# First g on VectorE, wqkv's low halves and fc2's maxima at other places, and q made with its units down the partitions

## Chip, core and metric

The kernel runs on one core of one Trainium2 chip. The metric is the device time of one execution in microseconds (us). Points in time are counted from the start of the profiled execution's span.

## The reference, cut to what matters

`x` is (4, 2048, 512). Both parts start from `xn`, the layer norm of `x`. Part one is a linear recurrence over the 2048 time steps, part two a feed-forward net with a layer norm of its own and quantised weights; the output is `x + s * silu(ffn(xn))`.

```python
q, k, v = xn @ Wq.T, xn @ Wk.T, xn @ Wv.T          # 128 units each
def step(M, qkv):                                    # over time
    r_t = q_t @ M.T
    M_new = 0.99 * M + v_t.T @ k_t / b
s = (r @ Wo.T) * sigmoid(gate)
h = layernorm(xn) * gamma + beta
y = silu(h @ dequant(fc1_q) + b1)                    # 512 -> 2048
z = y @ dequant(fc2_q) + b2                          # 2048 -> 512
out = x + s * silu(xn + 0.5 * z)
```

## The kernel before

**Tiling.** The 8192 rows are 16 chunks of 512 rows. A chunk is 4 tiles of 128 rows, each 32 time steps of the 4 sequences, so the recurrence is done tile by tile: within a tile by a masked 128x128 score matrix, between tiles by the memory `mem_t`. The normalised rows `g_rows` are turned by TensorE (line 410, the first chunk's by line 523) and split into two float16 halves `g_hi` and `g_lo`; `h_hi`, `h_lo` are the feed-forward input, split by GpSimd (lines 1016, 1020). The weights `wqkv` and `q2` are split into halves too.

**Slots.** The order of all work after the start is written out by hand as slots, 64 for a chunk, and every engine walks the same slots in its own queue, with semaphores between them. In each slot TensorE does one step of fc1 (`ffn1`, line 466, two matmuls of 512 columns) and one of fc2 (`ffn2`, line 484, two matmuls), which runs 16 slots behind. ScalarE rescales fc1's sum between steps (line 603) and makes the silu (line 610), VectorE splits it into `y_hi` and `y_lo` (lines 708, 713) and rescales fc2's sum (line 722). fc1 needs slots 0, 2, 4, 6 for the even blocks and 5, 7, 9, 11 for the odd ones.

**Side jobs.** `SIDE` places the recurrence between them. Tile i of a chunk has `qkv` at slot 1 + 12 i (line 427: 12 matmuls with 128 rows of g held and 384 columns of weights passing), `qkt` 4 slots later (lines 432 and 433: q and k transposed), `scores` at +7 (line 436), `read` at +10 (lines 443 to 445, where 443 waits for VectorE's `mask_scores`, line 697, at slot 9 + 12 i) and `wo` at +13 (line 451). The turns of the next chunk are at slots 51, 54, 56 and 59. ScalarE copies the results out one slot behind (`qkv_copy`, `qkt_copy`, `r_copy`, `s_copy`); the scale of a row goes into q, k and v there. Side jobs alternate between two PSUM banks, and each waits until the job two before it has been copied out.

**The start.** Before slot 0, VectorE takes the maxima of wqkv and of q1 (line 760, 2048 elements in 2.28 us), GpSimd works out the row scales (`rows`, lines 978 to 988) and normalises the first chunk (`normalise`, line 1004), TensorE turns it, ScalarE copies it out as `h_full` (line 565) and `g_hi` (line 556), and VectorE makes `g_lo` (line 692) and `wqkv_lo` (line 872). Slot 0 of TensorE waits for `q1_scale`; its first `qkv` waits for `wqkv_split` and for all of `g_lo`.

**fc2's weights.** They are converted in chunk 0, in 16 pieces that share the two buffers of `wide`: GpSimd widens piece n at slot 14 + 3 n (`q2_widen`, line 1031), VectorE rounds it a slot later (`q2_high`, line 796), GpSimd makes the rest at two slots later (`q2_low`, line 1036). First the scale must be there: VectorE's maxima at slots 0, 1, 5 and 9, `pick` at slot 12, `largest` and `q2_scale` at slot 13. The ratio rows of fc2 (`ratio2`, held at slot 2) go through DRAM. The next chunk's `rows` stand on GpSimd at slot 28 in chunk 0 and at slot 7 in the others.

## Time and profile before

| | us |
|---|---|
| median of 3 runs (1291.27 to 1292.08) | 1291.49 |
| the profiled execution | 1291.07 |
| its span, first to last instruction | 1289.2 |
| TensorE busy | 1204.1 (93%) |
| VectorE busy | 1132.0 (88%) |
| ScalarE busy | 906.9 (70%) |
| GpSimd busy | 805.4 (62%) |

TensorE's mean granted clock is 0.986 of full speed. In the chain of work that ended last, TensorE has 77% of the span, VectorE 11%, issue 5%, ScalarE 3%, GpSimd 3%. A matmul's duration overlaps with that of the next, so the pace of TensorE is read from the starts.

### The profile page before, as it was taken

The numbers are of one execution on the slowest core, as the hardware profiler recorded it, in microseconds if no ns is written. First come the engines' busy times: TensorE is split into PE (matmuls) and PEld (weight loads), VectorE is DVE, ScalarE is ACT, GpSimd is POOL, SyncE is SP. The second block draws the span as 40 slices with busy tenths as digits, with TensorE's granted clock in tenths as the row PEclk, the third lists the DMA queues.
The fourth block names the chain that finished last, engine by engine and source line by source line (L and its number), as shares of the span: only waits on it lengthen the run. The fifth ranks groups of instructions, "written<-read, shape, count | busy, mean of one in ns | idle before, by whom it ended". The sixth has DMA issues, their size and how long they took to land.

```text
span 1289.2 us, 18645 instructions
## 1 busy us (share of the span) xinstructions
PE 1204.1 (93%) x5900; PEld 608.0 (47%) x5900; DVE 1132.0 (88%) x1962; ACT 906.9 (70%) x1558; POOL 805.4 (62%) x766
## 2 busy tenths in 40 slices
...
DMA packets 41620, 65.68 MB, mean 51 GB/s; under 512 B 11696, under 2 KB 11952, under 8 KB 41008
## 3 DMA queue, kind: packets, MB, share of 16 engines
...
q10 hardware_dynamic: 288, 0.08, 0.0%
...
## 4 chain that ended last, share of the span: by engine, by line
PE 77%; DVE 11%; issue 5%; ACT 3%; POOL 3%; DMA 1%; SPq 0%; DVEq 0%; POOLq 0%; ACTq 0%
PE blk L466 28%; PE blk L484 27%; PE side L427 10%; DVE blk L722 5%; PE side L451 4%; DVE y_split L713 2%; PE side L443 2%; DVE y_split L708 1%; PE side L410 1%; DVE g_lo L692 1%; PE side L444 1%; PE side L445 1%; PE side L436 1%; POOL g_rows L1004 1%; ACT blk L603 1%
## 5 line engine op out<-in xcount | busy, mean ns | idle before, releaser
L722 DVE TENSOR_TENSOR blk<-blk,ratio_rows 128x512 f32<-128x512 f32 x960 | 644.9, 690 | 88.9 <-PE blk L484 85.3
L603 ACT ACTIVATE blk<-blk,ratio 128x512 f32<-128x512 f32 x768 | 508.1, 666 | 228.5 <-PE blk L466 218.6
L466 PE MATMUL blk<-h_split,q_sb 128*128 128x512 f16 x2048 | 613.8, 382 | 10.2 <-issue 4.9
L484 PE MATMUL blk<-w_sb,y_split 128*128 128x512 f16 x2048 | 610.6, 380 | 6.5 <-DVE blk L722 4.3
L484 PEld LDWEIGHTS blk<-w_sb,y_split 128*128 128x128 f16 x2048 | 199.4, 98 | 253.5 <-DVE blk L722 14.1
L466 PEld LDWEIGHTS blk<-h_split,q_sb 128*128 128x128 f16 x2048 | 196.3, 98 | 223.9 <-issue 36.3
L610 ACT ACTIVATE y_full<-blk,par,last 128x512 f32<-128x512 f32 x256 | 201.3, 786 | 112.4 <-PE blk L466 112.3
L713 DVE SCALAR_TENSOR_TENSOR y_split<-y_full,up,y_split 128x512 f16<-128x512 f32 x256 | 218.8, 855 | 0.0
L1016 POOL CAST h_split<-h_full 128x512 f16<-128x512 f32 x64 | 52.9, 826 | 251.5 <-ACT h_full L565 251.5
L708 DVE TENSOR_SCALAR y_split<-y_full,up 128x512 f16<-128x512 f32 x256 | 159.4, 623 | 5.0 <-ACT y_full L610 5.0
L1004 POOL TENSOR_SCALAR g_rows<-xt,mv,gs 128x512 f32<-128x512 f32 x64 | 141.5, 2218 | 0.1
L1061 POOL TENSOR_TENSOR z_rows<-z_rows,xz 128x512 f32<-128x512 f32 x62 | 92.4, 1499 | 49.2 <-DVE z_rows L727 47.9
L1067 POOL TENSOR_TENSOR z_rows<-z_rows,s_rows 128x512 f32<-128x512 f32 x62 | 91.8, 1480 | 34.6 <-ACT z_rows L618 34.6
L1056 POOL TENSOR_TENSOR xz<-xz,b_half 128x512 f32<-128x512 f32 x64 | 88.4, 1382 | 5.3
L1070 POOL TENSOR_TENSOR z_rows<-z_rows,x_again 128x512 f32<-128x512 f32 x62 | 84.8, 1367 | 4.9
L427 PE MATMUL side<-wqkv_hi,g_hi 128*128 128x384 f16 x256 | 85.1, 332 | 1.8 <-DVE g_lo L692 1.8
L427 PE MATMUL side<-wqkv_lo,g_hi 128*128 128x384 f16 x256 | 85.1, 332 | 0.0
L427 PE MATMUL side<-wqkv_hi,g_lo 128*128 128x384 f16 x256 | 85.1, 332 | 0.0
L1020 POOL TENSOR_TENSOR h_split<-h_full,h_split 128x512 f16<-128x512 f32 x64 | 76.6, 1197 | 5.2
L727 DVE SCALAR_TENSOR_TENSOR z_rows<-blk,unit,ratio_rows 128x512 f32<-128x512 f32 x64 | 47.6, 746 | 32.2 <-PE blk L484 32.2
L451 PE MATMUL side<-wo_sb,r_t 128*128 128x512 f32 x128 | 65.4, 592 | 0.0
L1053 POOL TENSOR_SCALAR xz<-x_again,row_z 128x512 f32<-128x512 f32 x64 | 60.8, 950 | 0.2 <-POOL z_rows L1061 0.2
...
## 6 DMA issues: line engine op xcount, KB each, us to landing
...
x_again<-in_x SPq DMA_DIRECT2D x256, 64.0 KB, 1.9
out<-z_rows SPq DMA_DIRECT2D x256, 64.0 KB, 1.7
w_sb<-in_q SPq DMA_DIRECT2D x4, 1024.0 KB, 13.8
ratio_rows<-ratio_dram SPq DMA_DIRECT2D x4, 1024.0 KB, 7.6
y_split<-in_q SPq DMA_DIRECT2D x1, 1024.0 KB, 10.5
h_split<-in_q SPq DMA_DIRECT2D x1, 1024.0 KB, 12.7
z_rows<-in_q SPq DMA_DIRECT2D x1, 1024.0 KB, 14.6
```

The source lines that it names most:

```text
L427: mm = pe.matmul(bank[:, 0:QKV], a[:, k, rows], w[:, k, :], start=(k == 0 and n == 0), stop=(k == KC - 1 and n == 2))
L451: pe.matmul(bank[:], r_t[:], wo_sb[:], start=True, stop=True).then_inc(wo_done, 1)
L466: mm = pe.matmul(blk[J % 2][:], q1_sb[:, g, j // 4, w, j % 4 * P:(j % 4 + 1) * P], a[:, c % 2, g, :], start=(g == 0 and n == 0), stop=(g = ...
L484: mm = pe.matmul(blk2[:, i, :], y[:, J % Y_RING, rows], w2_sb[:, j, part, :], start=(j == 0 and n == 0), stop=(j == FB - 1 and n == len(te ...
L603: act.activation(blk[J % 2][:], blk[J % 2][:], ACT.Copy, scale=ratio1[:, at:at + 1]).then_inc(blk_scaled, 1)
L610: act.activation(y_full[:, J % 2, :], blk[J % 2][:], ACT.Silu, bias=b1_c[:, j:j + 1], scale=last1[:, j:j + 1]).then_inc(silu_done, 1)
L708: dve.tensor_scalar(y_hi[:, J % Y_RING, :], y_full[:, J % 2, :], up_y, None, ALU.mult).then_inc(y_hi_done, 1)
L713: dve.scalar_tensor_tensor(y_lo[:, J % Y_RING, :], y_full[:, J % 2, :], up_y, y_hi[:, J % Y_RING, :], ALU.mult, ALU.subtract).then_inc(y_l ...
L722: dve.tensor_tensor(blk2[:, i, :], blk2[:, i, :], ratio2_rows[:, j, :], ALU.mult).then_inc(blk2_scaled, 1)
L1004: pool.tensor_scalar(g_rows[:, i, :], xt[:, i, :], mv[:, c % 2, i, 0:1], gs[:, c % 2, i:i + 1], ALU.subtract, ALU.mult).then_inc(g_done, 1)
L1061: pool.tensor_tensor(z_rows[:, i, :], z_rows[:, i, :], xz[:, i % 2, :], ALU.add).then_inc(z_sum, 1)
L1067: pool.tensor_tensor(z_rows[:, i, :], z_rows[:, i, :], s_rows[:, n % S_RING, :], ALU.mult).then_inc(z_mul, 1)
```

## The change

Four things are altered.

1. **First g.** Chunk 0's four normalisations leave GpSimd (line 1004) for VectorE (`first_normalise`), behind `pick(OF_WQKV)` and ahead of `largest(OF_WQKV)`.
2. **Order at the start.** ScalarE makes `wqkv_hi` behind `h_full` and `g_hi` instead of ahead; VectorE makes `wqkv_lo` last, behind the scale and flag of q1 and all four `g_lo`; q1's last maximum moves ahead of the first `g_lo`.
3. **fc2's weights.** Maxima at slots 0, 1, 3, 5, ratios at 6, scale at 10 and 11, pieces from slot 12 (each two slots earlier than before).
4. **q.** A new job `q` at slot 3 of each chunk makes q of all four tiles at once and already transposed: the weights are held and the 512 rows of g pass, 12 matmuls of 512 columns. `kv` takes the place of `qkv` with 256 columns, `kt` that of `qkt` with one transpose. q can't be scaled by row any more, so `s_copy` scales by a third row factor, which GpSimd makes in `row_scales`; `s_mask` and `r_t` share one buffer, so `mask_scores` waits for `wo_done`.

```diff
-QKV_LAG, QKT_LAG, R_LAG, S_LAG, GHIGH_LAG, HFULL_LAG = 1, 1, 1, 1, 1, 2
+Q_AT = 3
+Q_LAG, KV_LAG, KT_LAG, R_LAG, S_LAG, GHIGH_LAG, HFULL_LAG = 1, 1, 1, 1, 1, 1, 2
-RATIO2_AT, TOP_Q2_AT, Q2_SCALE_AT = 2, (0, 1, 5, 9), 12
-Q2_AT = tuple(14 + 3 * n for n in range(FB))
+RATIO2_AT, TOP_Q2_AT, Q2_SCALE_AT = 6, (0, 1, 3, 5), 10
+Q2_AT = tuple(12 + 3 * n for n in range(FB))
...
+                elif job == "q":
+                    for k in range(KC):
+                        for n, (a, w) in enumerate(((g_hi, wqkv_hi), (g_lo, wqkv_hi), (g_hi, wqkv_lo))):
+                            mm = pe.matmul(bank[:], w[:, k, 0:M], a[:, k, :],
+                                           start=(k == 0 and n == 0), stop=(k == KC - 1 and n == 2))
+                    mm.then_inc(q_done, 1)
...
-                            mm = pe.matmul(bank[:, 0:QKV], a[:, k, rows], w[:, k, :],
+                            mm = pe.matmul(bank[:, 0:2 * M], a[:, k, rows], w[:, k, M:],
...
-                    pe.transpose(bank[:, 0:P], qkv[:, i % 2, 0:M], ident[:])
-                    pe.transpose(bank[:, P:2 * P], qkv[:, i % 2, M:2 * M], ident[:]).then_inc(qkt_done, 1)
+                    pe.transpose(bank[:, 0:P], kv[:, i % 2, 0:M], ident[:]).then_inc(kt_done, 1)
...
+            def q_copy(c, i, bank):
+                act.wait_ge(q_done, c + 1)
+                wait(act, read_done, 4 * c)
+                act.activation(q_t[:], bank[:], ACT.Copy, scale=in_c[:, 0:1]).then_inc(q_out, 1)
...
-                act.activation(s_rows[:, n % S_RING, :], bank[:], ACT.Copy, scale=powers[:, 0:1]).then_inc(s_out, 1)
+                act.activation(s_rows[:, n % S_RING, :], bank[:], ACT.Copy,
+                               scale=row_c[:, c % 2, 2, i:i + 1]).then_inc(s_out, 1)
...
+            def first_normalise(i):
+                if i == 0:
+                    dve.wait_ge(rows_done, 1)
+                dve.tensor_scalar(g_rows[:, i, :], xt[:, i, :], mv[:, 0, i, 0:1],
+                                  gs[:, 0, i:i + 1], ALU.subtract, ALU.mult).then_inc(g_done, 1)
...
-                wait(dve, read_done, 4 * c + i)
+                wait(dve, wo_done, 4 * c + i)
...
             rows(0)
-            for i in range(NT):
-                normalise(0, i)
             row_scales(0)
```

VectorE in the start, around the maximum of wqkv; before:

```order
L764 TENSOR_REDUCE top_col<-side 32x1
L765 TENSOR_SCALAR top_diag<-ident,top_col 32x32
L771 TENSOR_REDUCE top_wqkv<-side 128x1
L856 TENSOR_SCALAR bound<-top_wqkv 128x1
L857 TENSOR_SCALAR pow<-bound 128x1
L859 RECIPROCAL up<-pow 128x1
L860 TENSOR_SCALAR up<-up 128x1
```

and after:

```order
L792 TENSOR_REDUCE top_col<-side 32x1
L793 TENSOR_SCALAR top_diag<-ident,top_col 32x32
L712 TENSOR_SCALAR g_rows<-xt,mv,gs 128x512 x4
L799 TENSOR_REDUCE top_wqkv<-side 128x1
L886 TENSOR_SCALAR bound<-top_wqkv 128x1
L887 TENSOR_SCALAR pow<-bound 128x1
L889 RECIPROCAL up<-pow 128x1
```

Four normalisations have come in between the maximum and its use; on GpSimd the same four rows are gone.

TensorE in chunk 0, from the end of the first tile's `qkv` (slot 1) to the scores (slot 8); before:

```order
L427 MATMUL side<-wqkv_hi,g_lo 128x384
L427 MATMUL side<-wqkv_lo,g_hi 128x384
L466 MATMUL blk<-h_split,q_sb 128x512 x6
L432 MATMUL side<-ident,qkv 128x128
L433 MATMUL side<-ident,qkv 128x128
L466 MATMUL blk<-h_split,q_sb 128x512 x6
L436 MATMUL side<-qk_t 128x128
```

and after, from the end of `kv` into the new job `q` (`blk` is fc1's sum, `side` the side jobs' banks):

```order
L439 MATMUL side<-wqkv_hi,g_lo 128x256
L439 MATMUL side<-wqkv_lo,g_hi 128x256
L479 MATMUL blk<-h_split,q_sb 128x512 x2
L428 MATMUL side<-g_hi,wqkv_hi 128x512
L428 MATMUL side<-g_lo,wqkv_hi 128x512
L428 MATMUL side<-g_hi,wqkv_lo 128x512
```

Each `qkv` has lost a third of its columns, and 12 matmuls of 512 columns stand at slot 3.

GpSimd in chunk 0, at the end of `rows` and `row_scales` of chunk 1 (slot 28); before:

```order
L988 TENSOR_TENSOR row_z<-v,row_const 128x4
L996 TENSOR_TENSOR row_c<-v,in_c 128x4 x2
L1031 TENSOR_SCALAR xz<-w_sb,up 128x512
L1036 TENSOR_TENSOR w_sb<-xz,w_sb 128x512
L1031 TENSOR_SCALAR xz<-w_sb,up 128x512
```

and after:

```order
L1018 TENSOR_TENSOR row_z<-v,row_const 128x4
L1026 TENSOR_TENSOR row_c<-v,in_c 128x4 x2
L1026 TENSOR_TENSOR row_c<-v,powers 128x4
L1065 TENSOR_TENSOR w_sb<-xz,w_sb 128x512
L1060 TENSOR_SCALAR xz<-w_sb,up 128x512
L1065 TENSOR_TENSOR w_sb<-xz,w_sb 128x512
```

Behind the row scales GpSimd now finishes a piece and then widens the next, where it widened one at once; that next widening is piece 6 and not piece 5.

## Rows read from the trace of the kernel before

**Rows 1.** Busy time per engine in 76 us of steady work: PE, PEld, DVE, ACT, POOL.

```profile
207.00:283.00 76.00, 74.83 (x375) 38.27 (x374) 68.50 (x119) 56.25 (x99) 49.83 (x47) 1.00 0.17 42
```

**Rows 2.** TensorE's waits from 200 to 1200: line, releaser, total us, times, longest.

```profile
PE side L443 <- issue: 7.7, 13, 0.6
```

**Rows 3.** TensorE in time, one chunk's start: start, duration, [idle before, releaser].

```profile
513.22 0.33 PE L427 MATMUL side<-wqkv_hi,g_hi 128*128 128x384 f16 x1
...
515.17 0.59 PE L466 MATMUL blk<-h_split,q_sb 128*128 128x512 f16 x2
...
518.71 0.27 PE L432 MATMUL side<-ident,qkv 128*128 128x128 f32 x1
...
518.93 0.59 PE L466 MATMUL blk<-h_split,q_sb 128*128 128x512 f16 x2
519.36 0.59 PE L484 MATMUL blk<-w_sb,y_split 128*128 128x512 f16 x2
...
523.90 0.59 PE L484 MATMUL blk<-w_sb,y_split 128*128 128x512 f16 x2
525.09 0.46 PE L443 MATMUL side<-qk_t,mem_t 128*128 128x128 f32 x2 [0.59 <-issue]
```

**Rows 4.** VectorE in time, the mask for that read.

```profile
524.71 0.28 DVE L697 TENSOR_TENSOR s_mask<-side,mask 128x128 f32<-128x128 f32 x1
```

**Rows 5.** Chain of waits, tiles 1 and 2 of chunk 0: start, us, piece.

```profile
57.55 3.84 PE side L427 x12
...
77.22 1.95 PE side L427 x12
```

**Rows 6.** All engines in time, the start.

```profile
17.54 8.27 POOL L1004 TENSOR_SCALAR g_rows<-xt,mv,gs 128x512 f32<-128x512 f32 x4
...
25.87 1.12 PE L523 MATMUL blk<-ident,g_rows 128*128 128x128 f32 x4 [0.94 <-POOL g_rows L1004]
27.29 0.61 POOL L1016 CAST h_split<-h_full 128x512 f16<-128x512 f32 x1 [1.16 <-ACT h_full L565]
...
27.81 0.69 DVE L692 TENSOR_TENSOR g_lo<-blk,g_hi 128x512 f16<-128x512 f32 x1 [3.94 <-ACT g_hi L556]
...
31.67 1.80 DVE L872 SCALAR_TENSOR_TENSOR wqkv_lo<-s_rows,up,wqkv_hi 128x1536 f16<-128x1536 f32 x1
...
34.40 0.15 DVE L882 TENSOR_SCALAR q_shift<-up 128x1 f32<-128x1 f32 x1
...
36.10 1.01 PE L466 MATMUL blk<-h_split,q_sb 128*128 128x512 f16 x2 [3.67 <-issue]
...
37.55 0.50 PE L427 MATMUL side<-wqkv_hi,g_hi 128*128 128x384 f16 x1 [0.44 <-DVE g_lo L692]
```

**Rows 7.** Page, costliest groups: VectorE's y_hi, count, busy us, mean ns.

```profile
L708 DVE TENSOR_SCALAR y_split<-y_full,up 128x512 f16<-128x512 f32 x256 | 159.4, 623 | 5.0 <-ACT y_full L610 5.0
```

**Rows 8.** All engines in time, slots 6 to 16 of chunk 0.

```profile
46.59 0.78 ACT L610 ACTIVATE y_full<-blk,par,last 128x512 f32<-128x512 f32 x1
...
55.96 0.63 PE L497 MATMUL blk<-top_diag,ones 32*128 32x32 f32 x2 [2.81 <-DVE top_diag L765]
...
64.72 0.59 PE L466 MATMUL blk<-h_split,q_sb 128*128 128x512 f16 x2 [1.19 <-issue]
```

**Rows 9.** Page, DMA issues: KB each, median us from issue to landing.

```profile
ratio_rows<-ratio_dram SPq DMA_DIRECT2D x4, 1024.0 KB, 7.6
```

**Rows 10.** All engines in time, slots 28 to 65 of chunk 0.

```profile
89.93 0.69 POOL L1031 TENSOR_SCALAR xz<-w_sb,up 128x512 f32<-128x512 int32 x1
...
90.65 0.43 DVE L796 CAST w_sb<-xz 128x512 f16<-128x512 f32 x1 [4.45 <-POOL xz L1031]
...
91.75 0.60 PE L484 MATMUL blk<-w_sb,y_split 128*128 128x512 f16 x2 [3.07 <-DVE blk L722]
...
94.76 0.77 PE L443 MATMUL side<-qk_t,mem_t 128*128 128x128 f32 x2 [2.41 <-issue]
...
137.82 0.32 PE L427 MATMUL side<-wqkv_hi,g_hi 128*128 128x384 f16 x1 [1.32 <-DVE g_lo L692]
```

More of the change, by code:

```diff
@@ L208, in build @@
         xz = sb("xz", [P, 2, H], F32)
-        qkv = sb("qkv", [P, 2, QKV], F32)
-        qk_t = sb("qk_t", [P, 2 * P], F32)
-        s_mask = sb("s_mask", [P, P], F32)
-        r_t = sb("r_t", [P, P], F32)
+        kv = sb("kv", [P, 2, 2 * M], F32)
+        q_t = sb("q_t", [P, T], F32)
+        k_t = sb("k_t", [P, P], F32)
+        s_mask = r_t = sb("s_mask", [P, P], F32)
         mem_t = sb("mem_t", [P, M], F32)
@@ L442, in run_side @@
                     wait(pe, mem_done, 4 * c + i)
-                    pe.matmul(bank[:, 0:P], mem_t[:], qk_t[:, 0:P], start=True, stop=False)
-                    pe.matmul(bank[:, 0:P], qkv[:, i % 2, 2 * M:3 * M], s_mask[:], start=False, stop=True)
-                    pe.matmul(bank[:, P:2 * P], qkv[:, i % 2, M:2 * M], qkv[:, i % 2, 2 * M:3 * M],
+                    pe.matmul(bank[:, 0:P], mem_t[:], q_t[:, i * P:(i + 1) * P], start=True, stop=False)
+                    pe.matmul(bank[:, 0:P], kv[:, i % 2, M:], s_mask[:], start=False, stop=True)
+                    pe.matmul(bank[:, P:2 * P], kv[:, i % 2, 0:M], kv[:, i % 2, M:],
                               start=True, stop=True).then_inc(read_done, 1)
@@ L589, in s_copy @@
                 n = 4 * c + i
-                if c == 0 and i == 0:
-                    act.wait_ge(decay_done, 1)
                 if n < S_RING:
@@ L637, in _ @@
                 q1_piece(n, 1.0, minus_point[:, 0:1])
-            act.wait_ge(wqkv_scale, 1)
-            act.activation(wqkv_hi[:], wqkv_in, ACT.Copy, scale=up_wqkv).then_inc(wqkv_hi_done, 1)
             for k in range(KC):
@@ L642, in _ @@
                 g_high(0, k, first_turn_bank[k])
+            act.wait_ge(wqkv_scale, 1)
+            act.activation(wqkv_hi[:], wqkv_in, ACT.Copy, scale=up_wqkv).then_inc(wqkv_hi_done, 1)
             act.wait_ge(q1_scale, 1)
@@ L661, in _ @@
                     q1_piece(FB // 2 + Q1_AT.index(G), up_q1, q1_shift[:, 0:1])
[L662 to L665 removed]
+                if at := job_behind(G, Q_LAG, "q"):
+                    q_copy(*at, side[JOB_BANK[G - Q_LAG]])
+                if at := job_behind(G, KV_LAG, "kv"):
+                    kv_copy(*at, side[JOB_BANK[G - KV_LAG]])
+                if at := job_behind(G, KT_LAG, "kt"):
+                    kt_copy(*at, side[JOB_BANK[G - KT_LAG]])
                 if at := job_behind(G, R_LAG, "read"):
@@ L854, in _ @@
             pick(OF_WQKV)
+            for i in range(NT):
+                first_normalise(i)
             largest(OF_WQKV, top_wqkv[:])
@@ L888, in _ @@
             g_low(0, 3, first_turn_bank[3])
+            dve.wait_ge(wqkv_hi_done, 1)
+            dve.scalar_tensor_tensor(wqkv_lo[:].rearrange("p k n -> p (k n)"),
+                                     wqkv_in.rearrange("p k n -> p (k n)"), up_wqkv,
+                                     wqkv_hi[:].rearrange("p k n -> p (k n)"), ALU.mult, ALU.subtract
+                                     ).then_inc(wqkv_split, 1)
             def q1_parts():
```

83 lines of the change are left out of this document (40 added, 43 removed).

## The prediction, made before the changed kernel ran

> **What bounds the kernel now.** I read the page's busy shares first, then the busy time by window, the waits of TensorE, one chunk of its timeline, and last the start. In 76 us of steady work TensorE is busy for 74.83, VectorE for 68.50, ScalarE for 56.25 and GpSimd for 49.83 [rows 1]: TensorE is the bound, and VectorE stands close behind it. So in chunks 1 to 15 a microsecond taken from TensorE's work comes off the end, as long as VectorE keeps up. The one named wait of any size there is that of the chunk's first read, 13 times, 7.7 us in all [rows 2]. Its cause is VectorE: the mask ends at 524.99 and the read starts at 525.09 [rows 3, 4]. VectorE is late there because the turns' low halves (slots 54 to 62) and the next chunk's statistics (slots 0 to 6) come on top of its usual work, while TensorE has only 1.95 us of side work in slots 1 to 4. The matmul ahead of the read started at 523.90, and a pair takes 0.43 (518.93 to 519.36), so the read could have started at 524.33: the wait costs 0.76 us a chunk [rows 3].
>
> Chunk 0 is another regime. Up to 37.55 the chain goes through GpSimd, ScalarE and VectorE, with TensorE waiting [rows 6]. From slot 12 to 65 fc2's weight pieces tie GpSimd and VectorE together, and TensorE runs dry several times [rows 8, 10]. After such gaps it runs at the lower of its two clock levels, 1.2 instead of 2.4 GHz: the 12 matmuls of tile 1, which followed a gap, took 3.84 us, the same 12 of tile 2 took 1.95 [rows 5].
>
> **A, start to slot 16 (gain 8, bounds 4 and 10).** *First g.* On GpSimd the four take 8.27 us from 17.54 [rows 6]. VectorE's nearest row is y_hi, a TENSOR_SCALAR of the same 512 elements with a mean of 0.62 [rows 7]. I take 0.5, bounds 0.4 and 1.0, so 1.6 to 4 us, and the first is there at about 18.1. Behind it the 16 turns take over: the last four took 1.12 [rows 6], about 0.23 each, so 3.6 for all, and the first bank is turned at about 21.4 instead of 26.4. *VectorE up to q1's flag (ends at 34.55).* Its queue gains four normalisations (+2.0), loses the 3.94 us wait ahead of the first g_lo, the 1.80 us of wqkv_lo [rows 6], and about 0.5 of waiting in pick: the flag comes some 4 us earlier, at 30.5, and slot 0 at about 32.1 instead of 36.10. GpSimd's h halves start when the row scales are through, 23.4 instead of 27.29 [rows 6], and end before that, so they don't decide. *First kv.* Behind the flag VectorE still has last1 (0.7), two g_lo (1.2) and now wqkv_lo (1.8): it is ready at 34.4. So kv starts 3.1 us earlier, not 5. Costed at nothing: wqkv_hi behind the g_hi on ScalarE, done at about 30, hidden by VectorE's maxima; were that cover gone, it would cost 1.6. *q in chunk 0.* 12 matmuls of 512 columns are 2.6 us at the higher level, 5.1 at the lower; I take 3.6, since TensorE has been busy for some microseconds by then. The first kv saves a third of about 3.9, 1.3. Together the first silu, at 46.59 [rows 8], comes about 1.7 earlier. *fc2's scale.* The maxima now end before slot 6, so the spread sits at slot 11 and not at 13. There it waits for VectorE, which has the ratios (2.4 us) and block 0's y in front; at the end of slot 11 the lead is 1.3. At slot 13 the wait of 2.81 and the spread of 0.63 are gone [rows 8], which is 3.4; and as there is no gap, tile 1's kv runs at the higher level with 256 columns, 1.3 instead of 3.84 [rows 5], 2.5; the other matmuls of slots 13 to 15 gain 0.8. Sum 1.3 + 3.4 + 2.5 + 0.8 = 8.0: the first matmul of slot 16 at 56.7 instead of 64.72 [rows 8]. SP's queue: the ratios are held at slot 6, so they leave at about 47.5 instead of 45.9 and, with 5 us for the way out and 7.6 for a quarter on the way back [rows 9], land at 58 to 60, while VectorE wants them at 57.5. That costs 0 to 2, which I leave in the lower bound.
>
> **B, slot 16 to the first kv of chunk 1 (gain 4, bounds 0 and 9).** Before, 64.72 to 137.82 [rows 8, 10]: 73.1 us, of which TensorE's own work is about 54 (49 slots of two pairs at 0.43, and 11.5 of side jobs). What stands out is slot 30: GpSimd's row arithmetic for chunk 1 lies ahead of piece 5, which it widens at 89.93; VectorE waits 4.45 for it, and TensorE 3.07 and 2.41 [rows 10], after which it runs at the lower level for a while. The change puts piece 5 ahead of that arithmetic, but then piece 6 waits for it and for the rest of piece 5 (1.16): I get a wait of 4.2 on VectorE one slot later. The stall is moved by a slot, not removed. What is gained is the slack of two slots for each piece (two waits of about 1 us at slots 20 and 24), and that slot. The third row factor adds 0.17 on GpSimd. The floor is an estimate: VectorE's work of about 58 us, and GpSimd's of about 60 with its waits for VectorE's halves, reckoned from its pieces (16 of about 2.5), the row arithmetic (6), four g (9) and four h (7); so more than 9 isn't there; nothing is the other end, if GpSimd sets the pace. With A, the first kv of chunk 1 starts at 125.8.
>
> **C, the work of TensorE per chunk (gain 0.36 in each of 15, 5.4).** A transpose costs half of 518.71 to 518.93, 0.11 [rows 3]: four fewer, -0.44. The 48 qkv matmuls cost (515.17 - 513.22) / 12 = 0.1625, 7.80. Now 48 kv and 12 q. q is 12 x 0.216 = 2.60. A kv of 256 columns has no row; from 384 to 512 columns it goes from 0.1625 to 0.216, so 0.109, and the transposes, each with a weight load of its own, show that 0.11 can be kept up [rows 3]: 5.28. Together 7.88, +0.08. Net -0.36.
>
> **D, the first read (gain 0.76 in each of 14, 10.6; bounds 0 and 14).** In slots 1 to 4 TensorE now has 1.3 (kv) and 2.6 (q) instead of 1.95, 1.95 more, all of it ahead of the read. VectorE has the same work there, so it makes up 1.95 on TensorE, more than the 0.76 that was lacking. The time comes back in tiles 1 to 3, 0.65 each. There VectorE has some 10.7 to 12 us of work per 12 slots against TensorE's 13.5; I give back 0.1 per chunk for small new waits at the later reads, 1.5. ScalarE: q_copy (0.68) at slot 4 has the pieces it replaces next to it; k_t and q_t are there by slot 8. The new wait of mask_scores for wo_done has nothing behind it: wo of the tile before is seven slots earlier. s_copy's new factor is made 50 slots ahead.
>
> **Sum.** 8 + 4 + 5.4 + 10.6 - 1.5 = 26.5, against the profiled execution's 1291.07: 1264.6. The median of the runs is 0.4 above that execution, so I say 1265.
>
> **Rivals.** *R1, the read's wait moves instead of going.* VectorE has 68.5 us of work and the chunk gets shorter; what it makes up by slot 9 it could lack at the turns or later reads. For it: VectorE's 90%. Against: the stretch from slot 13 to 50 has slack. Then D is nothing: 1291.1 - 17.4 = 1273.7.
> *R2, A's lead is eaten by slot 65.* GpSimd and VectorE pass 16 pieces to and fro and normalise; if their chain has a fixed end, 8 of the 12 are lost: 1272.6.
> *R3, slower: the weight load shows at 256 columns.* Each kv matmul has a load of its own. Where a load takes longer than what of it the matmul before covers, the rest falls on the path, 768 times. It decides from 26.5 / 768 = 0.035 us per matmul; a whole load, at most 0.11 by the transposes' pace [rows 3], makes 84 us, 1291.1 - 26.5 + 84 = 1349. Against it: two 128-column transposes with their loads took 0.22, and 384 columns took 0.1625, which leaves 0.0025 beside 384 / 2.4 GHz [rows 3].
> The Trainium skill (TensorE: Matmul & The Clock Gate, in Part 3, "The mechanism") says that a weight load overlaps with matmuls in flight only where their row groups differ; all loads here use all rows. By that rule no load would be hidden, before or after, and the 12 more loads a chunk would add about 1.3 us each chunk; by the rows it adds nothing. The trace of before disagrees with the rule, since its matmuls of 384 columns follow each other with no load between.
> *R4, the first g doesn't bring the start forward,* because VectorE's own chain to wqkv_lo ends no earlier (normalisations at 1.0 or beyond): A is lost, 1272.6.
> *R5, more:* chunk 0 near its floor and D whole, 1291.1 - 35 = 1256.
>
> **Chances.** Forecast 0.50, R1 0.22, R2 0.12, R3 0.05, R4 0.04, R5 0.07. The range takes in the forecast, R1, R2, R4 and most of R5: 1256 to 1276; outside stay R3 and sums of R1 with R2. A measurement of this kernel can't tell less than 0.2% (2.6 us) from no change. Only R1, R2 and R4 together would end there, 0.02. Faster 0.93, slower 0.05.
>
> **What would show it.** Right: the first turned bank read at about 21.5, first kv near 34.5, slot 16 near 57, chunk 1's first kv near 126; a wait of about 4 us on VectorE at slot 31; a chunk every 73.8 us; the kv matmuls 0.11 apart; no named wait at line 456. Wrong: kv matmuls 0.13 or more apart (R3), the waits at the read or at the turns unchanged in sum (R1), a lead at slot 16 that is smaller at chunk 1 (R2).

## The result, and the profile after

| | before | changed |
|---|---|---|
| median of the runs, us | 1291.38 (1290.48 to 1292.08, 4 runs) | 1283.63 (1282.58 to 1284.90, 4 runs) |
| span of the profiled execution, us | 1289.2 | 1283.1 |
| ratio of the times | | 0.9945, 95% interval 0.9933 to 0.9958 |

The change takes 0.55% off, 7.75 us. I had forecast 1265 and a range from 1256 to 1276: the sign was right, the forecast gain of 26.5 was more than three times too large, and the result lies outside the range. (One of the 13 runs of the kernel before that stand beside experiments 1 to 4 took 1904 us at a granted clock of 0.63; no ratio uses it.)

The spans differ by 6.1 us. Three landmarks split this against the sum of the prediction:

| stretch | before | changed | gain | forecast |
|---|---|---|---|---|
| start to slot 16 (A) | 64.72 | 61.95 | 2.8 | 8 |
| slot 16 to chunk 1's first kv (B) | 73.10 | 71.32 | 1.8 | 4 |
| chunk 1's first kv to the end (C and D) | 1151.4 | 1149.8 | 1.6 | 14.5 |

The steady work comes first, as [rows 1]: busy time per engine in the same 76 us (PE, PEld, DVE, ACT, POOL, then granted clock, DMA share, GB/s), and three of TensorE's largest waits over the whole span (total us, times, longest); the kernel before had, in the same view, the line that stands last.

```profile
207.00:283.00 76.00, 74.71 (x383) 38.91 (x381) 69.51 (x119) 55.92 (x99) 50.02 (x48) 1.00 0.17 42
```

```profile
PE side L456 <- issue: 21.2, 32, 5.6
...
PE blk L479 <- issue: 8.1, 2, 5.4
PE side L415 <- DVE g_lo L720: 5.5, 16, 1.7
```

```profile
PE side L443 <- issue: 13.2, 17, 2.4
```

TensorE is as busy as it was (74.71 against 74.83), and VectorE's busy time has risen from 68.50 to 69.51 with the same 119 rows of instructions. The wait at the read is still there, now at line 456, and it is longer: 32 times instead of 17, and 21.2 us instead of 13.2. The steady chunk, from one last turn to the next over 13 chunks, took 74.94 us before and takes 74.88 now. It was to be 73.8.

TensorE in time, one steady chunk: start, duration, what waits in brackets.

```profile
507.67 0.27 PE L439 MATMUL side<-wqkv_hi,g_hi 128*128 128x256 f16 x1
...
508.98 0.59 PE L479 MATMUL blk<-h_split,q_sb 128*128 128x512 f16 x2
...
510.70 0.38 PE L428 MATMUL side<-g_hi,wqkv_hi 128*128 128x512 f16 x1
...
513.29 0.59 PE L479 MATMUL blk<-h_split,q_sb 128*128 128x512 f16 x2
...
520.10 0.59 PE L497 MATMUL blk<-w_sb,y_split 128*128 128x512 f16 x2
520.72 0.46 PE L456 MATMUL side<-q_t,mem_t 128*128 128x128 f32 x2
...
535.47 0.46 PE L456 MATMUL side<-q_t,mem_t 128*128 128x128 f32 x2 [0.70 <-issue]
```

The twelve kv matmuls take (508.98 - 507.67) / 12 = 0.109 each, the twelve of q (513.29 - 510.70) / 12 = 0.216: TensorE's own work has shrunk as forecast. The first read is no longer named as a wait; it starts 0.19 behind the pair ahead of it (520.10 + 0.43 = 520.53), where 0.76 had been lost. But the second read, which had lost 0.07, now loses 0.87, and the third 0.34 instead of 0.23. Summed over a whole chunk, the time between TensorE's starts beyond the usual pace of each matmul was about 2.2 us and is about 2.6. So TensorE's work has fallen by about 0.4 us a chunk, and the waits have moved on by one tile and grown by nearly as much.

VectorE and GpSimd in time, ahead of that second read (L1082 and L1085 are `prepare`, L1090 is `add_z`, L1096 and L1099 are `output`):

```profile
526.97 0.77 POOL L1082 TENSOR_SCALAR xz<-x_again,row_z 128x512 f32<-128x512 f32 x1
...
527.83 1.27 POOL L1085 TENSOR_TENSOR xz<-xz,b_half 128x512 f32<-128x512 f32 x1
527.95 1.43 DVE L736 TENSOR_SCALAR y_split<-y_full,up 128x512 f16<-128x512 f32 x1
529.18 1.34 POOL L1090 TENSOR_TENSOR z_rows<-z_rows,xz 128x512 f32<-128x512 f32 x1
...
529.90 1.16 DVE L741 SCALAR_TENSOR_TENSOR y_split<-y_full,up,y_split 128x512 f16<-128x512 f32 x1
530.50 1.21 POOL L1082 TENSOR_SCALAR xz<-x_again,row_z 128x512 f32<-128x512 f32 x1
530.99 2.48 DVE L750 TENSOR_TENSOR blk<-blk,ratio_rows 128x512 f32<-128x512 f32 x4
...
533.38 1.20 DVE L736 TENSOR_SCALAR y_split<-y_full,up 128x512 f16<-128x512 f32 x1
...
535.10 0.28 DVE L725 TENSOR_TENSOR s_mask<-side,mask 128x128 f32<-128x128 f32 x1
```

From 527.95 to 541.8 VectorE is never idle. Its halves of y take 0.48 and 0.74 us in experiment 3, where GpSimd's chain for the output is cut short, and 1.43, 1.16 and 1.20 here, while GpSimd works through that chain. The mask comes at 535.10, and the read waits for it. The Trainium skill (SBUF — State Buffer, in "SBUF: two separate sides") says that VectorE and GpSimd share one pair of ports as an exclusive lock: a VectorE operation in a two-port mode or with two SBUF inputs and a GpSimd operation don't run at once, and the later of the two waits for the whole of the other. The stretched rows agree with that: the first ends at 529.38, 0.28 behind GpSimd's L1085 (529.10), the second at 531.06, 0.54 behind L1090 (530.52). The four rows of L750, which have only one of their inputs in SBUF, keep 0.6 us each beside GpSimd (530.99, 2.48 for four). That L736, with one input in SBUF, runs in a two-port mode, no row here says.

The trace of the kernel before had the tight place already. VectorE's mask for its second read, and the busy times from its first read to its second; below them those from the first to the second read of the changed kernel:

```profile
539.31 0.28 DVE L697 TENSOR_TENSOR s_mask<-side,mask 128x128 f32<-128x128 f32 x1
```

```profile
525.09:539.68 14.59, 14.59 (x72) 7.34 (x73) 12.42 (x20) 10.48 (x20) 13.88 (x17) 1.00 0.00 1
```

```profile
520.72:535.47 14.75, 13.99 (x71) 7.20 (x72) 13.28 (x20) 11.02 (x21) 14.04 (x18) 1.00 0.00 0
```

The mask ended at 539.59 and the read started at 539.68, so nothing of TensorE's work could be taken away there without a wait.

All engines in time, the start:

```profile
17.38 1.91 DVE L712 TENSOR_SCALAR g_rows<-xt,mv,gs 128x512 f32<-128x512 f32 x4
17.99 3.67 PE L536 MATMUL blk<-ident,g_rows 128*128 128x128 f32 x16
...
21.12 0.78 ACT L579 ACTIVATE h_full<-blk,beta_s,gamma_s 128x512 f32<-128x512 f32 x1 [2.43 <-PE blk L536]
...
30.40 0.15 DVE L907 TENSOR_SCALAR q_shift<-up 128x1 f32<-128x1 f32 x1
...
32.40 1.81 DVE L915 SCALAR_TENSOR_TENSOR wqkv_lo<-s_rows,up,wqkv_hi 128x1536 f16<-128x1536 f32 x1
...
34.35 0.37 PE L439 MATMUL side<-wqkv_hi,g_hi 128*128 128x256 f16 x1 [1.23 <-DVE wqkv_lo L915]
...
44.92 0.78 ACT L630 ACTIVATE y_full<-blk,par,last 128x512 f32<-128x512 f32 x1
```

These answer to [rows 6] and the first of [rows 8]. Every step is within 0.3 us of the forecast: the first bank read at 21.12 (21.4), the flag at 30.40 (30.5), the first kv at 34.35 (34.4), the first silu at 44.92 (forecast 1.7 before 46.59). Then, TensorE at slot 16, and the same for fc2's weights at slot 31, all engines:

```profile
55.98 0.59 PE L479 MATMUL blk<-h_split,q_sb 128*128 128x512 f16 x2
...
61.95 1.01 PE L479 MATMUL blk<-h_split,q_sb 128*128 128x512 f16 x2 [5.37 <-issue]
...
80.37 0.20 POOL L1008 TENSOR_TENSOR v<-mv,row_const 128x4 f32<-128x4 f32 x1
...
86.80 0.20 POOL L1026 TENSOR_TENSOR row_c<-v,powers 128x4 f32<-128x4 f32 x1
86.95 1.15 POOL L1065 TENSOR_TENSOR w_sb<-xz,w_sb 128x512 f16<-128x512 f32 x1
88.08 0.69 POOL L1060 TENSOR_SCALAR xz<-w_sb,up 128x512 f32<-128x512 int32 x1
88.81 0.43 DVE L824 CAST w_sb<-xz 128x512 f16<-128x512 f32 x1 [4.50 <-POOL xz L1060]
...
91.92 0.77 PE L456 MATMUL side<-q_t,mem_t 128*128 128x128 f32 x2 [5.58 <-issue]
```

```profile
L538 PEldq COMPARE_BRANCH  x1: 5535/5535/5535, 59.0 to 59.0; - x1
```

```profile
L551 PEldq COMPARE_BRANCH  x1: 5916/5916/5916, 55.9 to 55.9; - x1
```

The choice took 5.54 us in the kernel before as well. But TensorE still had matmuls queued up to 63.53, 4.5 us beyond the choice's start, half of tile 1's 12 at 1.2 GHz among them; in the changed kernel they end at 56.58, 0.7 us beyond it. The choice is reached 3.15 us earlier (55.87 for 59.02) and takes 0.38 longer, which is the 2.8 us by which slot 16 comes earlier.

At slot 31 GpSimd goes through the next chunk's row arithmetic from 80.37 to 87.0, VectorE waits 4.50 for the piece behind it, and TensorE 5.58, as much as the 3.07 and 2.41 of [rows 10] together.

### The profile page after: what moved, and what is told of

The parts are those of the page before. It is cut to its first block, busy times and chain, and to the rows that moved or that the text cites. A ratio compares the mean times of both kernels' runs of the same rounds, so it can differ in the third digit from the quotient of the medians.

```text
span 1283.1 us, 18950 instructions
## 1 busy us (share of the span) xinstructions
PE 1196.5 (93%) x6028; PEld 620.7 (48%) x6028; DVE 1144.5 (89%) x1966; ACT 904.8 (71%) x1574; POOL 798.6 (62%) x778
## 4 chain that ended last, share of the span: by engine, by line
PE 74%; DVE 12%; ACT 7%; issue 6%; DMA 1%; POOL 0%; SPq 0%; ACTq 0%; DVEq 0%; POOLq 0%
PE blk L479 27%; PE blk L497 25%; PE side L439 7%; DVE blk L750 5%; PE side L464 4%; PE side L428 3%; ACT blk L623 3%; PE side L456 2%; DVE y_split L741 2%; ACT z_rows L638 1%; DVE y_split L736 1%; PE side L415 1%; PE side L458 1%; PE side L457 1%; PE side L449 1%
## 5 line engine op out<-in xcount | busy, mean ns | idle before, releaser
L750 DVE TENSOR_TENSOR blk<-blk,ratio_rows 128x512 f32<-128x512 f32 x960 | 643.2, 688 | 88.4 <-PE blk L497 86.5
L736 DVE TENSOR_SCALAR y_split<-y_full,up 128x512 f16<-128x512 f32 x256 | 170.0, 664 | 0.0
L1033 POOL TENSOR_SCALAR g_rows<-xt,mv,gs 128x512 f32<-128x512 f32 x60 | 133.4, 2232 | 0.0
L1090 POOL TENSOR_TENSOR z_rows<-z_rows,xz 128x512 f32<-128x512 f32 x62 | 92.2, 1496 | 51.0 <-DVE z_rows L755 49.8
L1096 POOL TENSOR_TENSOR z_rows<-z_rows,s_rows 128x512 f32<-128x512 f32 x62 | 91.4, 1474 | 23.8 <-ACT z_rows L638 23.8
L1085 POOL TENSOR_TENSOR xz<-xz,b_half 128x512 f32<-128x512 f32 x64 | 88.8, 1388 | 5.3
L1099 POOL TENSOR_TENSOR z_rows<-z_rows,x_again 128x512 f32<-128x512 f32 x62 | 85.5, 1379 | 4.9
L439 PE MATMUL side<-wqkv_hi,g_hi 128*128 128x256 f16 x256 | 70.5, 275 | 1.5 <-DVE wqkv_lo L915 1.2
L439 PE MATMUL side<-wqkv_hi,g_lo 128*128 128x256 f16 x256 | 70.5, 275 | 0.0
L439 PE MATMUL side<-wqkv_lo,g_hi 128*128 128x256 f16 x256 | 70.5, 275 | 0.0
L464 PE MATMUL side<-wo_sb,s_mask 128*128 128x512 f32 x128 | 65.4, 592 | 0.0
L1082 POOL TENSOR_SCALAR xz<-x_again,row_z 128x512 f32<-128x512 f32 x64 | 60.2, 940 | 0.2 <-POOL z_rows L1090 0.2
## 6 DMA issues: line engine op xcount, KB each, us to landing
z_rows<-in_q SPq DMA_DIRECT2D x1, 1024.0 KB, 14.5
```

What stands on the lines that cost most here:

```text
L439: mm = pe.matmul(bank[:, 0:2 * M], a[:, k, rows], w[:, k, M:], start=(k == 0 and n == 0), stop=(k == KC - 1 and n == 2))
L464: pe.matmul(bank[:], r_t[:], wo_sb[:], start=True, stop=True).then_inc(wo_done, 1)
L736: dve.tensor_scalar(y_hi[:, J % Y_RING, :], y_full[:, J % 2, :], up_y, None, ALU.mult).then_inc(y_hi_done, 1)
L750: dve.tensor_tensor(blk2[:, i, :], blk2[:, i, :], ratio2_rows[:, j, :], ALU.mult).then_inc(blk2_scaled, 1)
L1033: pool.tensor_scalar(g_rows[:, i, :], xt[:, i, :], mv[:, c % 2, i, 0:1], gs[:, c % 2, i:i + 1], ALU.subtract, ALU.mult).then_inc(g_done, 1)
L1090: pool.tensor_tensor(z_rows[:, i, :], z_rows[:, i, :], xz[:, i % 2, :], ALU.add).then_inc(z_sum, 1)
```

## Experiments

Each lists its time, and the kernel before on the same chip beside it. The kernel before lies between 1291.17 and 1292.66 on these chips, and the changed kernel's 1283.63 was measured beside 1291.38, so differences of a microsecond between two kernels of different chips say nothing. Where one kernel holds several parts, "the changed kernel" is the one under study.

**1. Only the new q.** The kernel before with q's new layout alone; start, low halves and maxima as they were. Against the changed kernel, cut to fc2's slots:

```
-RATIO2_AT, TOP_Q2_AT, Q2_SCALE_AT = 6, (0, 1, 3, 5), 10
-Q2_AT = tuple(12 + 3 * n for n in range(FB))
+RATIO2_AT, TOP_Q2_AT, Q2_SCALE_AT = 2, (0, 1, 5, 9), 12
+Q2_AT = tuple(14 + 3 * n for n in range(FB))
```

> The kernel before with part 4 alone (q at slot 3, kv with 256 columns, one transpose); start and fc2's slots as before. Theory: in steady work it saves 0.41 us of matmuls a chunk but gives it back in waits, so a chunk stays at 74.9 us (74.93 before, 74.88 with the whole change), slot 16 starts later than before because the 2.6 to 5.1 us of q now stand in front of it, and the total is within 2 us of the kernel before. Rival (the q part is what gives the 6 to 8 us): 1283 to 1286.

Measured: 1289.23 us (1288.26 to 1290.16, 10 runs) against 1291.43; ratio 0.9982, interval 0.9973 to 0.9992. I had expected no more than 2 us. The steady chunk is 74.89, and slot 16 starts at 65.31, later than before, as expected. So q's new layout, to which I had given nearly 15 of the 26.5 us, brings 2.2.

**2. Only the start.** The other three parts without q's layout; against the changed kernel, in its core:

```
-Q_AT = 3
-SIDE = {Q_AT: ("q", 0)}
+SIDE = {}
```

> The kernel before with parts 1 to 3 alone (first g on VectorE, order at the start, fc2's slots); qkv as before. Theory: all of the gain comes from chunk 0, so this one is at 1281 to 1286, and its chunks take 74.93 us. Rival (gain belongs to q): 1289 to 1291. If the 5.37 us wait ahead of slot 16 comes from the ratio rows' transfer, it is here too, at 4 to 6 us.

Measured: 1284.34 us (1282.61 to 1285.20, 4 runs) against 1291.43; ratio 0.9940, interval 0.9922 to 0.9958. That is the whole gain of the change within the measurement. The two parts don't add: 2.2 and 7.1 alone, 7.7 together. Slot 16 starts at 60.84 behind a nameless wait of 5.55, so that wait doesn't hang on the layout of q.

**3. GpSimd's output chain on a quarter of the columns.** This leaves out three quarters of the columns of the five operations on `xz` and `z_rows` on GpSimd, and so a part of the output; two of the five:

```
-pool.tensor_tensor(xz[:, i % 2, :], xz[:, i % 2, :], b2_half[:], ALU.add).then_inc(xz_done, 1)
+pool.tensor_tensor(xz[:, i % 2, 0:P], xz[:, i % 2, 0:P], b2_half[:, 0:P], ALU.add).then_inc(xz_done, 1)
...
-pool.tensor_tensor(z_rows[:, i, :], z_rows[:, i, :], xz[:, i % 2, :], ALU.add).then_inc(z_sum, 1)
+pool.tensor_tensor(z_rows[:, i, 0:P], z_rows[:, i, 0:P], xz[:, i % 2, 0:P], ALU.add).then_inc(z_sum, 1)
```

> The changed kernel with GpSimd's five z operations per tile (scale of x, add of the bias, add of z, product with s, add of x) on 128 of 512 columns, so a part of the output is left out. Theory (VectorE is stretched by GpSimd in slots 13 to 35): the y operations there fall from 1.0 to 1.5 us to 0.48 and 0.74, the waits of 0.70 and 0.18 ahead of the second and third read go, and a chunk takes 73.6 to 74.1 us instead of 74.88. Rival (VectorE's own work is what holds, stretched or not): the waits stay above 0.5 us in sum and a chunk stays above 74.5.

Measured: 1263.47 us (one run) against 1291.43. The steady chunk is 73.82, and in the steady chunks no read is named as a wait. Its VectorE and TensorE in time, at the place of the second read:

```profile
523.02 0.48 DVE L736 TENSOR_SCALAR y_split<-y_full,up 128x512 f16<-128x512 f32 x1
...
524.01 0.74 DVE L741 SCALAR_TENSOR_TENSOR y_split<-y_full,up,y_split 128x512 f16<-128x512 f32 x1
...
527.67 0.48 DVE L736 TENSOR_SCALAR y_split<-y_full,up 128x512 f16<-128x512 f32 x1
...
529.67 0.38 PE L456 MATMUL side<-q_t,mem_t 128*128 128x128 f32 x2
```

VectorE's same instructions are back at 0.48 and 0.74, and the wait at the second read is gone. VectorE, slowed by GpSimd, is what holds the chunk at 74.9; without that neighbour the forecast of 73.8 holds to the tenth. The edit shortens GpSimd's own chain too, but in the changed kernel VectorE doesn't wait for that chain in the stretch in question: it is never idle there.

**4. fc2's ratios first.** The changed kernel with the ratios made, and so their rows sent, at slot 0 instead of 6:

```
-RATIO2_AT, TOP_Q2_AT, Q2_SCALE_AT = 6, (0, 1, 3, 5), 10
+RATIO2_AT, TOP_Q2_AT, Q2_SCALE_AT = 0, (0, 1, 3, 5), 10
```

> The changed kernel with the ratios of fc2 held at slot 0 instead of 6, so that their 4 MB of rows leave some 9 us earlier (about 44 instead of 52.9) and have landed when TensorE branches at 56.6. Theory (the wait of 5.37 us ahead of slot 16 is the branch's code, queued behind that transfer): the wait falls to 1 to 2 us, slot 16 starts at about 58, the total falls by 1 to 4 us. Rival (the wait has another cause, as the branch itself or GpSimd's pieces): it stays above 4 us and the total is that of the changed kernel.

Measured: 1279.87 us (1278.81 to 1281.06, 4 runs) against 1291.43; ratio 0.9909, interval 0.9891 to 0.9927: 3.8 us better than the changed kernel. The wait ahead of slot 16 is 3.68 instead of 5.37, where I had expected 1 to 2, and the choice takes 4.18 instead of 5.92. Shorter, not gone. In the profiled executions the wait gives 1.7 us, and the stretch from slot 16 to the last turn for chunk 1 another 1.5 (63.4 instead of 64.8), which wasn't taken apart.

**5. q in two halves.** The changed kernel with 256 of q's 512 columns at slot 3 and 256 at slot 19:

```
-Q_AT = 3
+Q_AT = (3, 19)
-SIDE = {Q_AT: ("q", 0)}
+SIDE = {at: ("q", n) for n, at in enumerate(Q_AT)}
```

> The changed kernel with q in two halves of 256 columns: tiles 0 and 1 at slot 3, tiles 2 and 3 at slot 19, where VectorE is the late one. Theory (the saved matmul time is lost as waits in slots 13 to 23, and the 1.3 us that leave slot 3 are still enough there): the wait of 0.70 us ahead of the second read goes, the one ahead of the first is 0.1 to 0.7, and a chunk takes 73.9 to 74.5 us instead of 74.88: 6 to 14 us less in all. Rival (a loop of fixed length, such as ScalarE's or the memory's chain, holds the chunk): 74.8 to 75.0, total within 2 us of the changed kernel.

Measured: 1269.98 us (1268.61 to 1270.31, 4 runs) against 1291.98; ratio 0.9828, interval 0.9812 to 0.9845. The steady chunk is 73.83, a little below the 73.9 that I had expected at the least; the second read has no wait left, the first starts 0.28 late and the third 0.34. The columns are the same, with 12 more matmuls of q and one more copy per chunk, and VectorE's halves of y still take 1.43 and 1.16 in the middle of the stretch. But 1.3 us of TensorE's work now stand between the first read and the second, where VectorE was behind, and no longer ahead of the first, where it wasn't. What the change takes off TensorE appears in the time as soon as the cover is spread.

**6. A mask buffer of its own.** In the change `s_mask` and `r_t` share a buffer, so that the mask waits for wo of the tile before. Undone:

```
-        s_mask = r_t = sb("s_mask", [P, P], F32)
+        s_mask = sb("s_mask", [P, P], F32)
+        r_t = sb("r_t", [P, P], F32)
...
-                wait(dve, wo_done, 4 * c + i)
+                wait(dve, read_done, 4 * c + i)
```

> The changed kernel with s_mask and r_t in buffers of their own again, the mask waiting for the read before as it did. Rival (the mask's new wait for wo is what moved the read's wait to tile 1): the 0.70 us go and a chunk takes 74.1 or less. Theory: the wait is VectorE's queue, nothing changes, 74.88.

Measured: 1282.18 us (one run) against 1291.98. The reads still wait 0.68 and 0.18, and the chunk is still 74.9. The added wait is not the cause.

**7. Experiments 4 and 5 together.** The changed kernel with the edits of both.

> The changed kernel with both: q in two halves at slots 3 and 19, and the ratios held at slot 0. Expected by the theories together: the sum of the two gains, 7 to 18 us below the changed kernel, 1266 to 1277. If they fall short of the sum, chunk 0's pieces take the earlier start back.

Measured: 1266.08 us (1265.19 to 1267.10, 4 runs) against 1291.98; ratio 0.9804, interval 0.9787 to 0.9820. That is 3.9 less than experiment 5, and experiment 4 had taken 3.8 off the changed kernel: the two add up.

**8. The ratio rows in quarters.** The changed kernel, with the second, third and fourth MB of ratio rows held back until 3, 5 and 8 of fc2's pieces are ready:

```
             for n in range(4):
+                if n:
+                    sp.wait_ge(q2_done, (0, 3, 5, 8)[n])
                 sp.dma_start(ratio2_rows[:, 4 * n:4 * n + 4, :], ratio2_dram[4 * n:4 * n + 4, :].partition_broadcast(P)
```

> Edit: the changed kernel, with only the first quarter of fc2's ratio rows (1 MB of 4 MB) sent at once; the other three leave when 3, 5 and 8 of fc2's weight pieces are ready. Theory Q (TensorE's fetch of its next code at slot 16 stands behind the 4 MB of ratio rows): the first quarter is through by about 58, so the issue wait ahead of the first fc1 matmul of slot 16, 5.37 in the changed kernel, shrinks to about 1.2 to 2, and slot 16 starts near 58.5 instead of 61.95. If GpSimd and VectorE let it pass on, the total falls by 1 to 3 us, to 1281 to 1283. Rival T (the code fetch itself takes that long after an idle-free approach, whatever the transfers do): the wait stays at 4.5 to 5.5 and the total at 1283.6. Chunk period 74.9 under both.

Measured: 1281.99 us (1281.60 to 1282.59, 4 runs) against 1291.17; ratio 0.9927, interval 0.9911 to 0.9944. The wait ahead of slot 16 is 5.01, what rival T expected; the time is what theory Q expected. But the one quarter was not through when TensorE came: it moved from 54.6 to 57.0. The experiment didn't part the two theories; experiment 11 does.

**9. VectorE's halves of the pieces later.** The changed kernel, with pieces 3 to 15 three slots behind GpSimd's widening on VectorE, and one slot more for the low half on GpSimd:

```
+Q2_HIGH_AT = tuple(at + (1 if n < 3 else 3) for n, at in enumerate(Q2_AT))
-                if G - 1 in Q2_AT:
+                if G in Q2_HIGH_AT:
...
-                if G - 2 in Q2_AT:
+                if G - 1 in Q2_HIGH_AT:
```

> Edit: the changed kernel, with VectorE's half of fc2's pieces 3 to 15 two slots later (three slots behind GpSimd's widening instead of one), and GpSimd's low half behind it. Theory S (the stall at slot 31 is VectorE standing in its queue for a widening that GpSimd does behind its row arithmetic, with the later y pieces queued behind it): the 4.50 us wait of VectorE and the 5.58 us of TensorE at slot 31 go to under 1.5; chunk 1's first kv comes 2 to 4 us earlier than 133.27, and the total is 1280 to 1282. Rival G (GpSimd's own work sets the pace of chunk 0 up to the turns): TensorE waits as much elsewhere, first kv of chunk 1 within 1 us of 133.3, total 1283 to 1284.5. Chunk period 74.9 under both.

Measured: 1279.47 us (1277.72 to 1280.80, 4 runs) against 1291.17; ratio 0.9910, interval 0.9893 to 0.9926. All its engines in time, at the former stall:

```profile
86.44 1.36 DVE L825 CAST w_sb<-xz 128x512 f16<-128x512 f32 x1 [1.45 <-POOL xz L1061]
...
87.67 0.59 PE L498 MATMUL blk<-w_sb,y_split 128*128 128x512 f16 x2 [1.24 <-POOL w_sb L1066]
```

TensorE's 5.58 have become 0.69 at the read and this 1.24, and VectorE's 4.50 have become 1.45. Chunk 1's first kv starts at 126.58, 6.7 us earlier than in the changed kernel, where I had expected 2 to 4; 2.1 of it was there at slot 16, which comes at 59.88 for a reason told below (the clock). From fc2's first matmul to chunk 1's last turn TensorE needs 58.9 us (60.69 to 119.54) instead of 64.0 (62.75 to 126.79). So the stall was VectorE standing in its queue for a piece that nobody needed yet, with the y pieces behind it. GpSimd's own work didn't set that pace.

**10. All of these.** Experiments 4, 5, 8 and 9 together:

> Edit: q in two halves at slots 3 and 19, fc2's ratios made at slot 0, the ratio rows sent in quarters and VectorE's halves of fc2's pieces three slots behind, all on the changed kernel. If theories Q and S hold and add to the version with the first two edits (1266.1): 1261 to 1265, period 73.83, first kv of chunk 1 at 124 to 127. If GpSimd sets the pace of chunk 0: 1265 to 1266.5, first kv of chunk 1 near 128.

Measured: 1260.40 us (1259.98 to 1260.49, 4 runs) against 1291.17; ratio 0.9758, interval 0.9741 to 0.9774. The steady chunk is 73.84, chunk 1's first kv starts at 123.72. It beats the kernel before by 2.4% and the changed one by 23 us: 14 x 1.04 = 14.6 in the steady chunks, and the rest mostly in chunk 0. I had expected 1261 to 1265 and the first kv from 124 to 127; both came out a little better.

**11. Ratios first, and in quarters.** Experiments 4 and 8 together, so that no transfer is on its way when TensorE comes to its next code:

> Edit: the changed kernel with both edits together: fc2's ratios made at slot 0, and only the first quarter of their rows (1 MB) sent at once. The 1 MB then moves from about 46 to 48.5, so no transfer runs when TensorE comes to its next code at about 54. In the runs so far the code packet landed 3 to 4 us behind the start of the last matmul ahead of it where 4 MB were in flight, at the very end of the transfer in four runs where that ended in time, and at 0 us in the two runs where the transfer was long over; TensorE went on 2.3 to 2.9 us behind the packet in all of them. Theory Q (the packet waits for the transfer's traffic): the packet lands at about 54, the wait ahead of slot 16 is 1.7 to 2.3 instead of 3.68 with the first edit alone and 5.01 with the second alone, slot 16 starts near 56.5, and the total is 1277 to 1280. Rival T (the packet is late whenever TensorE arrives early, whatever the traffic): the wait stays at 3.5 to 5 and slot 16 at 58 to 59.5.

Measured: 1278.72 us (1277.98 to 1281.02, 4 runs) against 1292.66; ratio 0.9899, interval 0.9883 to 0.9916. TensorE in time at slot 16:

```profile
54.04 0.59 PE L481 MATMUL blk<-h_split,q_sb 128*128 128x512 f16 x2
...
57.43 0.59 PE L481 MATMUL blk<-h_split,q_sb 128*128 128x512 f16 x2 [2.79 <-issue]
```

What the DMA queues moved between 54.8 and 55.0 (queue, kind: packets, MB, share of the 16 engines):

```profile
q8 instruction: 1, 0.02, 30.7%
```

This packet of code, 16 KB, is alone on the queues and takes 0.98 us (30.7% of 16 engines in 0.2 us). The rows of the choice in experiment 8 and here:

```profile
L553 PEldq COMPARE_BRANCH  x1: 5516/5516/5516, 54.1 to 54.1; - x1
```

```profile
L553 PEldq COMPARE_BRANCH  x1: 3300/3300/3300, 54.0 to 54.0; - x1
```

The two kernels reach the choice within 0.1 us of each other, and it takes 5.52 us with 1 MB on its way and 3.30 with none. The wait is 2.79, with the first edit alone it was 3.68, with the second alone 5.01, with neither 5.37. I had expected 1.7 to 2.3, so one part is the transfer's and another, larger than I gave it, is there without any transfer.

Nine kernels side by side. "Ahead" is the start of the last row of matmuls ahead of slot 16, "choice" the start of the choice and how long it takes; the packet's start is known to 0.2 us:

| kernel | ratio rows move | ahead | choice | code packet starts | slot 16 | packet to slot 16 |
|---|---|---|---|---|---|---|
| before | 52.2 to 62.1 | 62.94 | 59.02, 5.54 | 62.0 | 64.72 | 2.7 |
| experiment 1 | 52.6 to 62.9 | 60.22 | 59.19, 5.95 | 62.6 | 65.31 | 2.7 |
| experiment 4 | 45.3 to 55.4 | 53.78 | 53.72, 4.18 | 55.4 | 58.06 | 2.7 |
| experiment 8 | 54.6 to 57.0 | 54.14 | 54.07, 5.52 | 57.2 | 59.75 | 2.6 |
| changed | 54.0 to beyond 64 | 55.98 | 55.87, 5.92 | 59.2 | 61.95 | 2.8 |
| experiment 2 | 53.6 to 64.1 | 54.69 | 54.03, 6.64 | 58.2 | 60.84 | 2.6 |
| experiment 9 | 53.8 to beyond 64 | 53.78 | 53.70, 6.02 | 57.2 | 59.88 | 2.7 |
| experiment 11 | 45.0 to 48.0 | 54.04 | 53.96, 3.30 | 54.8 | 57.43 | 2.6 |
| experiment 7 | 44.4 to 54.6 | 56.61 | 55.58, 3.36 | 56.4 | 59.10 | 2.7 |

TensorE goes on 2.5 to 2.8 us behind the packet's start, in the other four kernels too; about 0.9 of that is the packet itself. The packet starts 0.9 to 1.5 us behind the choice where no ratio rows are on their way (experiments 7, 10 and 11), 1.8 behind it in experiment 4, where their transfer ends soon after, and 3.1 to 4.2 behind it in the nine kernels in which the rows are moving. So the traffic makes the choice longer, 5.5 to 6.6 us instead of 3.3 to 3.8. It did so in the kernel before as much as in the changed one; what differs between these two is how many matmuls lay over it. The Trainium skill (Runtime: NRT & Kernel Launch, in "Instruction fetch mechanics") says that code is fetched in blocks of 16 KiB over a DMA queue of the engine's own, and that a taken branch to a block that isn't loaded has to wait for it. Place and packet size agree; the times behind the packet and its delay behind other transfers are these rows' own. Why the delay is 3.1 in one kernel and 4.2 in another isn't settled.

## Why the prediction was wrong

**What bounds the kernel, and D with C: the step that failed.** I named VectorE as standing close behind TensorE and gave it a mean, 68.50 of 76, and from the mean I said that tiles 1 to 3 would take back time freely: "some 10.7 to 12 us of work per 12 slots against TensorE's 13.5". That step failed. Between the first and the second read VectorE was busy for 12.42 of 14.59 us in the kernel before and is for 13.28 of 14.75 now. Its halves of y cost 1.2 to 1.4 there, since GpSimd's output chain runs beside them, and from 527.95 on it is busy without a break. The trace of before showed it: the second read started 0.09 us behind its mask. So TensorE's 0.65 less work between the first read and the second came back as a wait of nearly the same size. The mechanism of D was right where I looked, 0.57 of 0.76 went at the first read; the second read took 0.80 of it back. In the range from 200 to 1200 us the named wait at the read went from 7.7 us in 13 times to 11.4 in 26. Rival R1, with 0.22, was the case that came about; it would have given 1273.7, and even that was too low, since R1 as I priced it let C's 0.36 per chunk stand. Where VectorE holds the chunk, not only what was to come from a wait is lost, but TensorE's saved work too. Experiments 3 and 5 show this from both sides: 73.82 with VectorE's neighbour gone, 73.83 with the cover spread, against my 73.8.

**C, the work itself.** Right: kv 0.109, q 0.216, a transpose 0.11, all as forecast. R3, the one rival that ended slower, fell: kv matmuls with a weight load of their own follow each other at 0.109. The rule of the Trainium skill (TensorE: Matmul & The Clock Gate, in Part 3, "The mechanism"), that loads overlap only with matmuls of other row groups, disagrees with this trace as with that of before: all rows are used, and no load shows. The same section also says that a load into the background weight buffer is pulled ahead of matmuls in flight; with that the traces agree, and by it the prediction's 1.3 us a chunk would not arise.

**A, start to slot 16: 2.8 instead of 8.** All terms up to the first silu hold to 0.3 us. Two things were missing. The first is the choice ahead of slot 16. I had a row, 1.19 in [rows 8], and carried it over as a constant. It was the uncovered end of a choice of 5.54 us. TensorE's matmuls end 6.95 us earlier (56.58 for 63.53), but the choice is reached only 3.15 earlier, and before, all matmuls from 59.02 to 63.53 had lain over it, more than half of the 3.84 us of tile 1's `qkv` among them. So the 2.5 and 0.8 that I gave to slots 13 to 15 could reach slot 16 only in part. In the sum this is 5.37 - 1.19 = 4.2 of the 5.2 us that A fell short. The ratio rows' transfer lengthens the choice by some 2 us (experiments 8 and 11), but in both kernels. I had looked at that very transfer, and asked only who wants its data. The second is the clock. Busy times and granted clock between 50 and 54 us, first the changed kernel, then experiment 9, whose instructions are the same up to there:

```profile
50.00:54.00 4.00, 4.00 (x18) 2.66 (x17) 1.23 (x8) 1.99 (x4) 0.69 (x1) 0.61 0.02 4
```

```profile
50.00:54.00 4.00, 4.00 (x26) 2.38 (x25) 2.12 (x8) 3.61 (x8) 0.69 (x1) 1.00 0.10 20
```

The changed kernel's profiled execution ran most of this stretch at 1.2 GHz, and its last matmuls ahead of slot 16 start at 55.98; that of experiment 9 ran it at 2.4 GHz, and there they start at 53.78. The forecast comes to 55.1 for them, and the 0.9 us between is the rest of A's shortfall; which clock an execution gets there was luck. The changed kernel's own runs fall into pairs, 1282.58 and 1282.60, 1284.67 and 1284.90, some 2.2 apart, about as much; that this is the same event wasn't tested. Its median lies between.

**B, slot 16 to chunk 1: 1.8 instead of 4.** The point of it was right: the stall moved by one slot, VectorE waits 4.50 where I had 4.2. TensorE lost the same there, 5.58 in one piece instead of 3.07 and 2.41. The term that fell short is the slack of two slots for the earlier pieces. TensorE's two waits for them, some 2 us, are gone as I had counted, but the first 15 us behind slot 16 are no faster. Before, then changed, as [rows 1]:

```profile
64.72:80.00 15.28, 13.18 (x67) 6.70 (x68) 12.82 (x24) 10.10 (x18) 6.33 (x8) 1.00 0.07 19
```

```profile
61.95:77.20 15.25, 14.40 (x65) 7.32 (x66) 12.39 (x23) 9.03 (x16) 5.89 (x6) 0.84 0.20 78
```

Behind the idle 5.37 us the granted clock is 0.84 there instead of 1.00, and TensorE is busy for 1.2 us more with about the same matmuls. That this is what took the gain is read from these rows and not tested. R2 came near in time, but its sign wasn't there: the lead of 2.8 us at slot 16 had not shrunk at chunk 1, it was 4.6; and experiment 9 shows that GpSimd's chain isn't the fixed end I feared there.

**R4** fell with A's first half, **R5** with all. The range was too narrow because its cases were taken as separate: the text leaves sums of R1 with R2 outside, and R1 with more than half of A and half of B lost is what happened.
